# Lag attention's weights folded about 127.5, and the router's weights loaded during lag attention

## The reference, cut to what matters

```
x = x + tanh(g_xattn[0]) * lag_attention(layernorm(x), ctx, ctx)
x = x + tanh(g_ffn[0])   * experts(layernorm(x), gate_w, u, g, d)     # top 2 of 16
x = x + tanh(g_xattn[1]) * context_attention(layernorm(x), ctx, Wq, bq, Wk, bk)
x = x + tanh(g_ffn[1])   * quantised_ffn(layernorm(x), ...)

# lag_attention, per batch and column:
corr  = ifft(fft(q) * conj(fft(k)))          # 256 lags
w, idx = top_k(corr, 11);  w = softmax(w)
out[p] = sum_i w[i] * v[min(idx[i] + p, 255)]
```

## Time and profile before

| | us |
|---|---|
| three runs: lowest, median, highest | 1376.68, 1379.06, 1380.38 |
| the profiled execution | 1376.35 |
| its span, first to last instruction | 1374.6 |

### The profile page before, as it was taken

The page is one execution under the profiler, slowest core; times in us unless marked ns, Lnnn a source line. Parts: engine busy times, 40 slices in busy tenths (PEclk is TensorE's granted clock), DMA queues, the critical chain, the costliest instruction groups (busy, mean ns, idle before and its releaser), DMA issues. The chain is left out here.

```text
span 1374.6 us, 20874 instructions
## 1 busy us (share of the span) xinstructions
PE 1259.7 (92%) x6498; PEld 857.0 (62%) x6498; DVE 779.1 (57%) x2009; ACT 501.8 (37%) x875; POOL 579.4 (42%) x964
## 2 busy tenths in 40 slices
PE   4899999999977999999999998999999999858786
PEld 2354544545433955448887787888888898535443
DVE  3878888888774572005533333444454443368895
ACT  2544444444432600013322222232222322178884
POOL 5676867768653000003222221523212231168885
PEclk9999999999998999999999999999999999979999
DMA  5210211402001800416777874526334331121111
GB/s 198 89 66 31 92 61 45 184 15 88 35 0 47 324 1 7 144 59 243 256 250 249 275 260 158 191 85 134 107 110 123 94 103 50 62 69 46 61 61 77
DMA packets 52481, 156.38 MB, mean 114 GB/s; under 512 B 5952, under 2 KB 16192, under 8 KB 52288
## 3 DMA queue, kind: packets, MB, share of 16 engines
q1 hardware_dynamic: 39152, 113.60, 23.2%
q0 software_dynamic: 13264, 41.95, 10.7%
HBM read 113.06 MB, written 45.61 MB: 115 GB/s over the span
## 5 line engine op out<-in xcount | busy, mean ns | idle before, releaser
L1213 PEld LDWEIGHTS ex_bank<-ex_xT,ex_gu 128*112 128x112 f32 x1248 | 140.5, 177 | 24.9 <-issue 23.9
L1213 PE MATMUL ex_bank<-ex_xT,ex_gu 128*112 128x128 f32 x1248 | 143.6, 273 | 2.7 <-issue 1.8
L44 PE MATMUL xa_bank<-fT_high,M_hi 128*128 128x256 f32 x512 | 143.9, 281 | 0.0
L46 PE MATMUL xa_bank<-fT_high,M_lo 128*128 128x256 f32 x512 | 142.9, 279 | 0.0
L45 PE MATMUL xa_bank<-fT_low,M_hi 128*128 128x256 f32 x512 | 142.9, 279 | 0.0
L52 PE MATMUL la_bank<-la_osum,la_tab 128*128 128x512 f32 x256 | 120.6, 616 | 13.1 <-POOL la_osum L295 11.9
L295 POOL TENSOR_TENSOR la_osum<-la_oprod 128x512 f32<-128x512 f32 x64 | 80.2, 1273 | 96.1 <-DVE la_oprod L481 96.1
L1077 POOL TENSOR_TENSOR ex_small<-listed,ex_small 128x1 int32<-128x1 int32 x42 | 15.4, 368 | 225.0 <-DVE Wk L1155 224.9
L44 PEld LDWEIGHTS xa_bank<-fT_high,M_hi 128*128 128x128 f32 x512 | 96.5, 189 | 0.3
L46 PEld LDWEIGHTS xa_bank<-fT_high,M_lo 128*128 128x128 f32 x512 | 96.6, 189 | 0.0
L45 PEld LDWEIGHTS xa_bank<-fT_low,M_hi 128*128 128x128 f32 x512 | 96.3, 188 | 0.0
(11 more groups left out here) (281 smaller groups left out, 2807.0 us busy)
## 6 DMA issues: line engine op xcount, KB each, us to landing
produced<-Wk SPq DMA_DIRECT2D x39, 512.0 KB
ex_gu<-in_gate_up SPq DMA_DIRECT2D x16, 896.0 KB
X<-in_x SPq DMA_DIRECT2D x8, 1024.0 KB, 7.5
la_v_raw<-in_ctx SPq DMA_DIRECT2D x16, 512.0 KB, 4.0
produced<-la_zeros SPq DMA_DIRECT2D x16, 512.0 KB, 4.8
normal<-rt_xn SPq DMA_DIRECT2D x16, 512.0 KB, 5.4
fT<-in_ctx_T SPq DMA_DIRECT2D x8, 1024.0 KB, 5.4
xa_f<-in_ctx SPq DMA_DIRECT2D x8, 1024.0 KB, 4.9
```

The lines of the kernel that those rows point to most:

```text
L44: pe.matmul(out, a[0], b[0], start=first, stop=False)
L46: return pe.matmul(out, a[1], b[0], start=False, stop=last)
L1213: m = pe.matmul(bank[half][0:INTER, 0:P], gu[:, slot, at:at + INTER], xT[:, k, :], start=(k == 0), stop=(k == KD - 1))
```

## The change

The fold is put about 127.5: lag 128 + i goes with lag 127 - i, so that every lag has a partner. The tables are made for that (half positions for the weights, whole ones for the way back), and lose two of their 128x128 parts, one in each of the two transfers of the table. `weight_spectra` has four products in place of six, `w_halves` loses its copy and works on 128 columns of each group in place of 127. The router's weights get a home that is allocated before lag attention, and are loaded there, behind Wq on SP's queue; `route` no longer loads them or waits for them. To make room, the identity in `experts` moves into a part of Wk's buffer that is no longer read there.

```diff
     last = np.zeros((2, P, P))
...
-    last[2, 0] = sign
-    lags = kinds(p)
+    lags = kinds(p + 0.5)
...
-    found = np.concatenate([P + np.arange(P), (P - np.arange(P)) % P])[None, :]
+    found = np.concatenate([P + np.arange(P), P - 1 - np.arange(P)])[None, :]
...
-ROWS_AT, LAST_AT, LAGS_AT, LAG_AT, POS_AT, SIGN_AT = 0, 4 * P, 7 * P, 11 * P, 11 * P + 2 * L, 19 * P + 2 * L
-TABLE_COLS = SIGN_AT + P
+ROWS_AT, LAST_AT, LAGS_AT, LAG_AT, POS_AT = 0, 4 * P, 6 * P, 10 * P, 10 * P + 2 * L
+TABLE_COLS = POS_AT + 8 * P
...
             sp.dma_start(Wq_home[:], Wq.rearrange("(k p) n -> p k n", p=P)).then_inc(s["Wq_in"], 16)
+            sp.dma_start(gw[:], gate_wT.rearrange("(k p) e -> p k e", p=P)).then_inc(s["gw_in"], 16)
...
             sp.wait_ge(s["Wq_in"], 16)
+            sp.wait_ge(s["gw_in"], 16)
...
-                a, b = wt[:, two, 1:P], wt[:, two, P + 1:L]
-                pool.tensor_tensor(w_less[:, two, 1:P], a, b, ALU.subtract).then_inc(s["w_fold"], 1)
-                pool.tensor_copy(w_less[:, two, 0:1], wt[:, two, P:P + 1]).then_inc(s["w_fold"], 1)
+                a, b = wt[:, two, 0:P], wt[:, two, P:L]
+                pool.tensor_tensor(w_less[:, two, :], a, b, ALU.subtract).then_inc(s["w_fold"], 1)
                 pool.tensor_tensor(a, a, b, ALU.add).then_inc(s["w_fold"], 1)
...
-                full_product(pe, bank[4][:], lags_t(0), more, True, False)
-                full_product(pe, bank[4][:], last_t(2), less, False, True)
+                full_product(pe, bank[4][:], lags_t(0), more)
                 at_least(pe, s["added1"], u)
-                full_product(pe, bank[5][:], lags_t(1), less, True, False)
-                full_product(pe, bank[5][:], sign_t, more, False, True).then_inc(s["wspec"], 1)
+                full_product(pe, bank[5][:], lags_t(1), less).then_inc(s["wspec"], 1)
...
         def _(sp):
-            sp.dma_start(gw[:], gate_wT.rearrange("(k p) e -> p k e", p=P)).then_inc(s["gw_in"], 16)
             sp.dma_start(b_raw[:, 0, :], bk).then_inc(s["b_in"], 16)
...
             pe.wait_ge(s["consts"], 3)
-            pe.wait_ge(s["gw_in"], 16)
...
-        ident = sb("ident", [P, P])
+        ident = W[1][:, 6, 0:P]
...
+            gw = projection.enter_context(nc.sbuf_tensor("router", [P, KD, EXPERTS], F32))
```

More of the change, by code:

```diff
@@ L70, in fourier_tables @@
     k = np.arange(P)[None, :].astype(np.float64)
-    sign = (-1.0) ** np.arange(P)
     def kinds(at):
@@ L77, in fourier_tables @@
     rows[:, 1, 0] = np.sin(np.pi * middle[:, 0])
-    last = np.zeros((3, P, P))
+    last = np.zeros((2, P, P))
     last[0, 0, 0] = L
     last[1, 0] = -2 * rows[:, 2].sum(0)
-    last[2, 0] = sign
-    lags = kinds(p)
-    lags[:, 1, 0] = 0
-    lags[0, 1, 0] = 1
-    lags[0, 3] = -sign
-    found = np.concatenate([P + np.arange(P), (P - np.arange(P)) % P])[None, :]
+    lags = kinds(p + 0.5)
+    lags[:, 1, 0] = np.sin(np.pi * (p[:, 0] + 0.5))
+    found = np.concatenate([P + np.arange(P), P - 1 - np.arange(P)])[None, :]
     angle = 2 * np.pi * p * found / L
@@ L91, in fourier_tables @@
     pos = []
-    for at in (p + 0.5, L - 0.5 - p):
+    for at in (p, L - 1 - p):
         one = kinds(at).transpose(1, 2, 0) * 2
         one[0, 0] = 1
-        one[1, 0] = -np.sin(np.pi * at[:, 0])
+        one[1, 0] = -np.cos(np.pi * at[:, 0])
         pos.append(one / (2 * L))
@@ L99, in fourier_tables, with lag_attention @@
     parts = [rows.reshape(P, -1), *last, lags.reshape(P, -1), lag.transpose(1, 0, 2).reshape(P, -1),
-             pos.transpose(2, 0, 1, 3).reshape(P, -1), sign[:, None] * (k == 0)]
+             pos.transpose(2, 0, 1, 3).reshape(P, -1)]
     return np.concatenate(parts, 1).astype(np.float32)
-ROWS_AT, LAST_AT, LAGS_AT, LAG_AT, POS_AT, SIGN_AT = 0, 4 * P, 7 * P, 11 * P, 11 * P + 2 * L, 19 * P + 2 * L
-TABLE_COLS = SIGN_AT + P
+ROWS_AT, LAST_AT, LAGS_AT, LAG_AT, POS_AT = 0, 4 * P, 6 * P, 10 * P, 10 * P + 2 * L
+TABLE_COLS = POS_AT + 8 * P
 def mirrored(x):
     return np.concatenate([x[:, :P], x[:, P:][:, ::-1]], 1)
-def lag_attention(nc, x, ctx, gate, tables, Wq, Wq_home, X, scales_after, produced):
+def lag_attention(nc, x, ctx, gate, tables, Wq, Wq_home, X, scales_after, produced, gate_wT, gw):
     C = 512
@@ L170, in pos_t @@
             return table(POS_AT + (2 * kind + j) * P, P)
-        sign_t = table(SIGN_AT, P)
-        names = """tab_in tab_rest gate_in Wq_in zeroed filled consts dchain
+        names = """gw_in tab_in tab_rest gate_in Wq_in zeroed filled consts dchain
                    q_ready spec_q spec_v1 spec_v2 v_ev1 v_ev2 prods sums added0 added1
@@ L558, in turn_weights @@
             def turn_weights(u):
-                at_least(pe, s["w_fold"], 6 * u + 6)
+                at_least(pe, s["w_fold"], 4 * u + 4)
                 at_least(pe, s["oprods"], 8 * u)
@@ L702, in merged_product, with route @@
     return last
-def route(nc, gate_wT, X, norm, normal, listed, slots, weights, first_tile, Wk, W, M32, bk, bq,
+def route(nc, gw, X, norm, normal, listed, slots, weights, first_tile, Wk, W, M32, bk, bq,
           shift, key_bias, constant):
@@ L725, in route @@
         xnT = [turned_rows[:, i, :, :] for i in range(2)]
-        gw = sb("gw", [P, KD, EXPERTS])
         ident = sb("ident", [P, P])
@@ L754, in route @@
         key_sum = sb("key_sum", [P, KD])
-        names = "gw_in consts turned xnT_act xnT_dve logits one xn_ready chain sums_pe slots_ready ex_ready gap_ready hot list_pe b_in wk_in dot by_bias columns key_sum key_hi m_pe m_out".split()
+        names = "consts turned xnT_act xnT_dve logits one xn_ready chain sums_pe slots_ready ex_ready gap_ready hot list_pe b_in wk_in dot by_bias columns key_sum key_hi m_pe m_out".split()
         s = {n: sem(n) for n in names}
@@ L1886, in build @@
             M_hi, Wq_home = with_guest("M_hi", "Wq")
-            lag_attention(nc, x, ctx, g_xattn, tables, Wq, Wq_home, X, running, produced)
+            gw = projection.enter_context(nc.sbuf_tensor("router", [P, KD, EXPERTS], F32))
+            lag_attention(nc, x, ctx, g_xattn, tables, Wq, Wq_home, X, running, produced, router_T, gw)
             M_lo, M32 = with_guest("M_lo", "M32")
@@ L1901, in build @@
                 fT, fT_parts, xT = quarter("fT", 1), [quarter("fT_high", 2, F32R), quarter("fT_low", 1, F32R)], quarter("xT", 3)
-                route(nc, router_T, X, running, normal, listed, slots, weights, first_tile, Wk, W, M32, bk, bq,
+                route(nc, gw, X, running, normal, listed, slots, weights, first_tile, Wk, W, M32, bk, bq,
                       shift, key_bias, constant)
```

## The result

The changed kernel was slower: 1402.38 us, the median of four runs (1400.10 to 1402.98), against 1378.14 for the kernel before beside it, a ratio of 1.0171 with an interval of 1.0152 to 1.0191. The forecast was 1375.8, its range 1370 to 1381. One thing must be said ahead of the rest: this kernel has two times, since in ten further runs of the same code six took 1400.0 to 1403.6 us and four 1371.8 to 1374.3. The profiled execution shown here took 1402.25, its span is 1400.5.

What follows compares the result with a forecast made beforehand. The prediction took a ring of waits through PE, DVE and POOL in lag attention, not PE alone, as the bound. Terms 0 + 1.7 + 1.4 + 0.2 = 3.3 us off the median 1379.06 gave 1375.8 us, range 1370 to 1381.

Steps and rivals of the forecast that it cites:

- the router's weights: Start of `route`: with the weights already loaded, PE's first transpose starts 1.4 us sooner and the gain stays; bounds 0 to 1.6.
- The clock's rival: Lag attention's loop: PE's longer stops make its clock fall in each unit, giving 1399 us; chance 0.07.
- Units 0 to 14: Lag attention: two products fewer in W gain 0, since P0 still waits for the same sums; bounds 0 and 25.8 us.
- Unit 15 and the end of lag attention: Last unit: `o_products` waits for W there, so W's two products fewer gain 1.72 us; bounds 0.9 to 2.6.
- The whole fold: Lag attention and tables: the fold's terms together, 1.7 us from unit 15 and 0.2 from the table's first part.
- The table's first part: Start of the kernel: a transfer of 384 KB instead of 448 lets ACT's tanh start 0.2 us sooner; bounds 0 and 0.9.
- SP: SP's queue behind Wq: the router's load, issued in 0.39 us, is hidden while SP waits for PE; cost 0.
- POOL's copy: Lag attention: dropping 28 copies, 5.3 us of POOL, costs and gains 0, within 0.3 us either way.
- the sum of 3.3 us: Whole kernel: gains of 0 + 1.7 + 1.4 + 0.2 us, taken off the median of 1379.06.
- The first rival: Lag attention: PE is the bound after all, so units 0 to 14 gain too, 29.1 us in all, 1350; chance 0.12.
- the rings: Lag attention: a closed chain of waits sets the period, 24.67 us: P0, C, T, P1, `add`, lags, `o_products`, `o_sum`, P0.

Runs made afterwards that it cites:

- fold_only: The changed kernel, but with the router's weights loaded in `route` and waited for there; 1375.12 us, ratio 0.9975 against the kernel before.
- two_tiles: The changed kernel, with PE waiting in `route` for two normalised tiles before its first transposes; 1374.77 us, ratio 0.9978 against the kernel before.
- before_early: The kernel before, with each product of P0 waiting for its own sum (the first for two) instead of all four; 1370.67 us, ratio 0.9950.
- router_two: `router_only` with PE waiting in `route` for two normalised tiles before its first transposes; 1378.27 us, ratio 1.0003 against the kernel before.
- warm: The changed kernel plus three products nobody reads, between the last P and `route`'s first transpose; 1373.12 us, ratio 0.9968 against the kernel before.
- router_warm: `router_only` plus three products nobody reads, between the last P and `route`'s first transpose; 1376.69 us, ratio 0.9987 against the kernel before.
- router_only: The changed kernel with the fold taken back (old tables, `w_halves` and W), early load of the router's weights kept; 1405.3 us, ratio 1.0198 against the kernel before.

## Why the prediction was wrong

**The failed step** is the router's weights, and in it the sentence "The gain stays, because PE is busy nearly throughout `route`". The 1.4 us in front of the first transpose came exactly (4.67 to 3.26 us, for the reason given). What was left out is PE's clock behind it. The kernel before entered the loop behind a stretch at half clock that ended at 446.5, and the prediction had those transposes at half clock in front of it (3.86 us for 17, in the earlier trace rows) without asking what brought the clock back, and what the loop would cost if it didn't come back. The term was +1.4; it measured -27 or so in the runs with the half clock. The price could have been bounded from the kernel before: 14 tiles of 2.29 us, with PE busy throughout, cost at most 32 us more at half the rate.

**The clock's rival had the right cause in the wrong place.** It put the fall into the lag attention's new pauses of 1.8 us. There the clock is 1.00 from 54 to 400 us; that part was settled as forecast. That its price, 1399, lies near the measured 1402 is luck: it was summed from 15 units that didn't lose anything. The rule of the Trainium skill that the prediction set beside it (TensorE: Matmul & The Clock Gate, section "HAM oscillation — how this bites in real kernels") speaks of a loop that stops for its data in each round, and for longer than PE's 1.8 us. No run here shows that: the loop that ran at half clock was one in which PE never stopped.

**The rest held.** Units 0 to 14: forecast 0, measured 24.67 - 24.64 = 0.03 us in the unit shown, and none over all of them: unit 15's W starts at 418.71, before at 418.57. Unit 15 and the end of lag attention: forecast 1.7, its end came 2.4 us earlier, within the bounds of 0.9 to 2.6; part of it is the clock, since the last P's took 8.70 us in place of 9.54. The whole fold: `fold_only` is 3.5 us faster than before (1.6 to 5.2 by its interval), forecast 1.9. The table's first part: forecast 0.2 sooner; the tanh stands at 9.88 us in place of 9.53, and since the traces with the old table have it anywhere between 9.53 and 10.21, that term can't be seen at all. SP: the issue of the router's load took 1.86 us at 238.60 in place of 0.39, and was still hidden. POOL's copy: nothing, as taken. Where the clock came back, the sum of 3.3 us was right in size: 0.9969 of before in four runs of the changed kernel is 4.3 us (1.4 to 7.0 by its interval), 0.9978 of `two_tiles` 3.0 (1.2 to 4.7).

**The first rival**, PE as the bound, is refuted by the 1.78 us in front of P0. It is half true in `before_early`: with P0's wait gone, PE's own work is the next bound, and only 0.37 us a unit behind.

## What to carry to other kernels

Before a start is moved earlier, look at PE's granted clock on both sides of it in the trace: a stage that is bound by small products may depend on the clock being up when it begins, and its price at the lower level is in the rows already. Two cheap guards held here in every run: to let the first work wait until twice as much of it is there, so that it starts later and in one piece (`two_tiles`, `router_two`), or to fill the idle time ahead with products that nobody reads (`warm`, `router_warm`). One piece by itself was no guard (`router_only`). An engine's freed time is worth what the rings through it give back: after each wait that is shortened, look for the ring that closes next, and in it for the wait that ends last.

## What the runs showed of the hardware

In this case PE's busy share in the profile didn't tell its clock. PE was busy for all of 71.6 us at 1.2 GHz in the router's loop (transposes of 128x128 between products of 128x16), and the clock rose only when the loop was over and the products of 128x512 had begun (the first at 507.54, the clock 1.00 from 511.5). The same loop, entered at 2.4 GHz, stayed there for 34 us, while transposes were among its work. In the kernel before the clock then fell at 480.6, PE still without a stop, in the last 34 products of 128x16, behind the last transpose (PE's timeline, then a stretch):

```profile
477.92 4.83 PE L979 MATMUL rt_bank<-rt_gw,rt_xnT 128*128 128x16 f32 x34
```
```profile
481.00:487.00 6.00, 6.00 (x15) 3.42 (x15) 4.15 (x50) 0.00 (x0) 0.00 (x0) 0.50 0.00 0
```

That the clock's rows are real is borne out by another engine: ACT's copies follow each other by 4.27 us in the one and 2.29 in the other. The Trainium skill (TensorE: Matmul & The Clock Gate, section "Seeing it yourself") warns that the clock's events in a trace may not be reliable; in this case they and the durations agree.

One stage could run at either level throughout, then, and which of them it takes can change from run to run of the same code, by 26 to 32 us in 1375. A median of four runs hid that here, and ten runs showed it.
